# Second batch's long-chunk convolution moved to TensorE as diagonal products, its pointwise part ahead of the first q, k, v, and the third batch's taps next on VectorE

## The reference

```
h = depthwise_conv(x, w_dw, 7 taps, SAME) + b_dw        # along the tokens, channel by channel
h = relu(w_pw @ h + b_pw); h = max over token pairs     # 1024 -> 512 tokens
y = real(fft2(h)); h = layernorm(y) * gamma + beta      # "front"
n = layernorm(h)
q, k, v = n @ Wq.T, n @ Wk.T, n @ Wv.T                  # 12 heads of 16 dims
h = h + causal_linear_attention(taylor_exp(q), taylor_exp(k), v) @ Wo.T
n = layernorm(h)
h = h + top-1 mixture of 8 experts(n) + scan features over the 512 tokens
```

## Time and profile before

| | |
|---|---|
| timed runs | 442.24, 436.63, 442.59 us; median 442.24 |
| profiled execution, its own time | 429.96 us |
| span of its instructions | 428.2 us |
| TensorE busy | 373.9 us, 87% |
| VectorE busy | 271.1 us, 63% |
| ScalarE busy | 150.1 us, 35% |
| GpSimd busy | 91.2 us, 21% |
| mean granted TensorE clock | 0.937 |

### The profile page before, as it was taken

One profiled execution on the slowest core, in us unless ns is written; L12 is line 12 of the kernel. 1 busy time (PEld: TensorE's weight loads), 2 busy tenths in 40 slices (PEclk: granted clock), 3 DMA queues, 4 the chain that ended last, 5 costly groups with the idle time before them and its releaser, 6 DMA issues.

```text
span 428.2 us, 7994 instructions
## 1 busy us (share of the span) xinstructions
PE 373.9 (87%) x2820; PEld 265.8 (62%) x2821; DVE 271.1 (63%) x866; ACT 150.1 (35%) x299; POOL 91.2 (21%) x128
## 2 busy tenths in 40 slices
PE   7999899889898888988988997889799999998273
PEld 4486657436374354743665535689699899887252
DVE  6689703999198992987024386738556655565783
ACT  1010120773106732067434461354333443342000
POOL 1000000451003520034101241400634433341100
PEclk9999899999899999999996899969999999999656
DMA  8667120000300000086002001120241111113504
GB/s 269 196 215 263 44 55 0 2 2 2 100 0 2 1 2 2 0 331 210 2 2 86 2 2 73 51 61 2 83 141 43 53 45 51 46 51 56 165 3 147
DMA packets 21571, 30.58 MB, mean 71 GB/s; under 512 B 9876, under 2 KB 18132, under 8 KB 21028
## 3 DMA queue, kind: packets, MB, share of 16 engines
q1 hardware_dynamic: 17812, 24.02, 17.5%
q0 software_dynamic: 2208, 5.29, 4.3%
q10 hardware_dynamic: 1520, 0.86, 0.7%
HBM read 24.20 MB, written 5.96 MB: 70 GB/s over the span
## 4 chain that ended last, share of the span: by engine, by line
PE 66%; DVE 14%; ACT 7%; issue 5%; DMA 3%; POOL 3%; DVEq 0%; ACTq 0%; POOLq 0%
PE upper L1630 10%; PE ring L1616 7%; PE upper L1479 5%; PE ring L1463 4%; PE ring L1620 4%; ACT probs L639 4%; PE ring L1372 4%; POOL probs L569 3%; PE upper L1307 2%; PE ring L1378 2%; PE ring L1353 2%; PE ring L1319 2%; PE upper L1535 2%; PE upper L1396 2%; PE ring L1358 2%
## 5 line engine op out<-in xcount | busy, mean ns | idle before, releaser
L569 POOL TENSOR_SCALAR_AFFINE_SELECT probs<-probs 128x256 f32<-128x256 f32 (+1 forms) x72 | 43.4, 604 | 212.9 <-ACT probs L639 211.8
L639 ACT ACTIVATE probs<-ring,ones 128x768 f32<-128x768 f32 (+1 forms) x54 | 52.0, 995 | 23.3 <-PE ring L1463 16.9
L721 ACT ACTIVATE probs<-ring,qk 128x128 f32<-128x128 f32 x138 | 38.2, 378 | 55.4 <-PE ring L1620 30.2
L1630 PE MATMUL upper<-w,probs 128*128 x276 | 51.8, 339 | 3.1 <-DVE probs L1105 1.8
L1630 PEld LDWEIGHTS upper<-w,probs 128*128 128x128 f32 x276 | 46.1, 196 | 5.2 <-issue 4.9
L1479 PE MATMUL upper<-probs,va 128*32 128x512 f32 (+3 forms) x384 | 34.9, 459 | 12.6 <-POOL probs L569 12.6
L1463 PE MATMUL ring<-qk 32*128 32x512 f32 (+3 forms) x276 | 43.0, 520 | 3.1 <-ACT probs L639 3.1
L770 DVE SCALAR_TENSOR_TENSOR wide<-w,wdw,wide 128x512 f32<-128x512 f32 (+1 forms) x42 | 41.1, 1020 | 0.6
L585 POOL DMA_INDIRECT ffn_by_token<-probs,target x23 | 22.5, 979 | 72.3 <-DVE probs L1113 71.1
L1616 PE MATMUL ring<-xsT,qk 128*128 128x128 f32 x276 | 35.9, 280 | 0.6 <-ACT xsT L713 0.6
L1463 PEld LDWEIGHTS ring<-qk 32*128 32x128 f32 x276 | 19.9, 193 | 25.3 <-ACT probs L639 18.9
(11 more groups left out here) (324 smaller groups left out, 624.7 us busy)
## 6 DMA issues: line engine op xcount, KB each, us to landing
w<-in_w SPq DMA_DIRECT2D x1, 4608.0 KB, 15.8
w1a<-in_w1a SPq DMA_DIRECT2D x1, 3072.0 KB, 10.5
w<-in_x SPq DMA_DIRECT2D x4, 512.0 KB, 3.9
w<-in_x SPq DMA_DIRECT2D x8, 256.0 KB, 5.0
w1b<-in_w1b SPq DMA_DIRECT2D x1, 1536.0 KB, 13.8
tokens<-x_all SPq DMA_DIRECT2D x4, 384.0 KB, 8.7
x_all<-ffn_by_token SPq DMA_DIRECT2D x4, 384.0 KB, 5.0
wide<-scores_linear SPq DMA_DIRECT2D x1, 1024.0 KB, 5.3
```

Of the source, the lines that this page charges most:

```text
L569: nc.gpsimd.affine_select(diag, diag, heads + [[1, P]], ALU.is_ge, minus_one, base=0, channel_multiplier=-1).then_inc(p_ready, 1)
L639: nc.scalar.activation(squares(n), score_bank(b, n)[:, :, 0:unit_width(n)], ACT.Square, bias=ones[:, 0:1], scale=0.25).then_inc(sq_done, 1)
L721: nc.scalar.activation(hT[slot][:, c, :], ring[slot][:, c % 2, P * (c // 2):P * (c // 2) + P], ACT.Gelu_apprx_tanh, bias=b1_col[slot][:, c ...
L1630: last = nc.tensor.matmul(att[2][:, 0:D], hT[slot][:, c, :], w2[:, bass.ds((e * HC + c) * D, D)], start=(c == 0), stop=(c == HC - 1))
```

## The change

VectorE builds a second set of seven diagonal matrices (`taps_long`) while it waits for the first pointwise result. TensorE computes batch 1's long chunk as 14 diagonal products (seven taps by two halves of the tokens) into `ring[0]`, behind `transform(0)` and ahead of the short chunk's seven. ScalarE adds the bias and writes `conv`, and raises `conv_done` by two. Both halves of `convolve(1)` leave VectorE. `pointwise(1)` goes to the PSUM pairs of `upper` instead of `ring`, and stands ahead of `project(0)`; the 56 fillers become 8, the 20 behind `pointwise(1)` go. `convolve(2)` moves on VectorE from between two of batch 0's attention sums to right behind `pool(1)`.

```diff
+        def point_banks(b):
+            return (ring[0][:, :, :], ring[1][:, 0, :]) if b != 1 else (upper[:, 0:2, :], upper[:, 2, :])
...
-        taps = probs[:, 0:TAPS * P].rearrange("p (k c) -> p k c", k=TAPS)
+        taps, taps_long = (probs[:, TAPS * P * i:TAPS * P * i + TAPS * P].rearrange("p (k c) -> p k c", k=TAPS)
+                           for i in range(2))
...
-        WARM_PROJECT, WARM_EXPERTS, WARM_FEATURES, WARM_ROWS = 56, 32, 14, 10
+        WARM_EXPERTS, WARM_FEATURES, WARM_ROWS = 32, 14, 10
...  ScalarE
             def project(b):
                 if b == 0:
                     copy_taps(1)
+                    act.wait_ge(long_sums_done, 1)
+                    nc.scalar.activation(conv, ring[0][:, :, :].rearrange("p h n -> p (h n)"), ACT.Identity,
+                                         bias=vec2[:, 0, 0:1]).then_inc(conv_done, 2)
...  VectorE, pool(b)
+                if b == 0:
+                    nc.vector.tensor_tensor(taps_long, ident[:, None, :].to_broadcast([P, TAPS, P]),
+                                            wdw[:, 0, :, None].to_broadcast([P, TAPS, P]), ALU.mult
+                                            ).then_inc(long_taps_ready, 1)
                 dve.wait_ge(pw_done, 2 * b + 1)
...  VectorE
             def front(b):
                 pool(b)
-                if b == 0:
-                    convolve(1, (0,))
+                if b == 1:
+                    convolve(2)
                 if b >= 2:
                     add_attended(b - 2)
                     normalise_again(b - 2)
                 untangle(b)
                 normalise(b)
-                if b == 0:
-                    convolve(1, (1,))
-                else:
+                if b > 0:
                     sums(b - 1, 1)
-                    if b < B - 1:
-                        convolve(b + 1)
+                    if b == 2:
+                        convolve(3)
                     sums(b - 1, 2)
...  TensorE
             def pointwise(b):
-                if b > 0:
+                if b == 1:
+                    pe.wait_ge(tap_sums_copied, 2)
+                if b > 1:
                     pe.wait_ge(gh_copied, 2 * b)
...
             def transform(b):
...
+                if b == 1:
+                    pe.wait_ge(qk_copied, KEY_BLOCKS)
+                    pe.wait_ge(v_copied, 1)
                 pe.wait_ge(pool_done, 8 * b + 4)
...
+            def sum_long_taps():
+                pe.wait_ge(long_taps_ready, 1)
+                for tap in range(TAPS):
+                    for h in range(2):
+                        last = nc.tensor.matmul(ring[0][:, h, :], taps_long[:, tap, :],
+                                                xin[:, 0, tap + 512 * h:tap + 512 * h + 512],
+                                                start=(tap == 0), stop=(tap == TAPS - 1))
+                last.then_inc(long_sums_done, 1)
...
             transform(0)
             pe.wait_ge(s_x, 96)
+            sum_long_taps()
             sum_taps(1)
             pe.wait_ge(y_done, 1)
-            keep_clock(WARM_PROJECT)
+            keep_clock(8, misc)
+            pointwise(1)
             pe.wait_ge(s_wa, 16 * len(ATTN))
             project(0)
-            pointwise(1)
-            keep_clock(WARM_FOLD)
             transform(1)
             attend(0)
             project(1)
```

More of the change, by code:

```diff
@@ L331, in build @@
         conv_done = sem("conv_done")
+        long_taps_ready, long_sums_done = sem("long_taps_ready"), sem("long_sums_done")
         taps_ready, tap_sums_done, tap_sums_copied = sem("taps_ready"), sem("tap_sums_done"), sem("tap_sums_copied")
@@ L812, in pool @@
                     dve.wait_ge(col_done, 2 * b)
-                gather(pooled[:, :, 0:even_n], ring[0][:, :, :].rearrange("p h (n two) -> p h n two", two=2), 0)
+                long, short = point_banks(b)
+                gather(pooled[:, :, 0:even_n], long.rearrange("p h (n two) -> p h n two", two=2), 0)
                 for h in range(2):
@@ L816, in pool @@
                 dve.wait_ge(pw_done, 2 * b + 2)
-                gather(pooled_s[:, 0:even_n], in_pairs(ring[1][:, 0, :]), 1)
+                gather(pooled_s[:, 0:even_n], in_pairs(short), 1)
                 for h in range(2):
@@ L1317, in pointwise @@
                 pe.wait_ge(conv_done, 2 * b + 2)
+                long, short = point_banks(b)
                 for h in range(2):
-                    nc.tensor.matmul(ring[0][:, h, :], wpw[:, 0, 0:P], of_parity(conv, h), start=True, stop=False)
+                    nc.tensor.matmul(long[:, h, :], wpw[:, 0, 0:P], of_parity(conv, h), start=True, stop=False)
                 if b < 2:
@@ L1322, in pointwise @@
                 for h in range(2):
-                    last = nc.tensor.matmul(ring[0][:, h, :], wpw[rows_of(h), 1, 0:P], conv_s[rows_of(h), :],
+                    last = nc.tensor.matmul(long[:, h, :], wpw[rows_of(h), 1, 0:P], conv_s[rows_of(h), :],
                                             start=False, stop=True)
@@ L1326, in pointwise @@
                 for h in range(2):
-                    nc.tensor.matmul(ring[1][rows_of(h), 0, :], wpw[:, 0, P:D], of_parity(conv, h), start=True, stop=False)
+                    nc.tensor.matmul(short[rows_of(h), :], wpw[:, 0, P:D], of_parity(conv, h), start=True, stop=False)
                 for h in range(2):
-                    last = nc.tensor.matmul(ring[1][rows_of(h), 0, :], wpw[rows_of(h), 1, P:D], conv_s[rows_of(h), :],
+                    last = nc.tensor.matmul(short[rows_of(h), :], wpw[rows_of(h), 1, P:D], conv_s[rows_of(h), :],
                                             start=False, stop=True)
```

## The result

The changed kernel takes 445.24 us (median of four runs, 440.0 to 448.31) against 439.44 of the kernel before beside it (433.03 to 442.59): ratio 1.0197, 95% interval 1.0116 to 1.0277. The ratio leaves disturbed runs out, so it isn't the quotient of the medians. The forecast was 444.2, +0.5%.

The account below looks back on a forecast made before the run. TensorE was taken to bound the kernel, VectorE to wait. transform(1) 2.7 us late less 0.7 in attend(0) made 2.0 us slower, put on the timed median of 442.24: 444.2, range 435 to 451.

Parts of the forecast that it names:

- transform(1): TensorE's start of batch 1's transform: at 70.3 instead of 67.61, 2.7 us late.
- Long sums: TensorE behind transform(0): 28 counted products added on the path at 0.453 each, 12.7 us.
- The new wait: TensorE before pointwise(1), for ScalarE's two copies: 2.0 us, bounds 1.7 and 2.4, about 1.1 us of it idle.
- Pointwise: pointwise(1) on TensorE, moved ahead of project(0): 5.1 us, 52.2 to 57.3.
- project(0): TensorE behind pointwise(1): 13.05 us instead of 14.6, with 1.56 us of low clock regained.
- kept-dip rival: Clock dip stays in project(0), or one its size (1.56) comes in the pointwise part: 3.6 us slower, 445.8; chance 0.28.
- The slow rival: Clock falls at ScalarE's two copies, before pointwise(1), and stays low: 8.7 us slower, 450.9; chance 0.12.
- Taps of batch 2: convolve(2) on VectorE: 13.7 us, from 60.0 to 73.7, with 3.9 us margin at untangle(1).
- late-convolution rival: Batch 2's x lands more than 5.3 us late, pushing batch 1's normalisation on VectorE: 446 to 449; chance 0.03.
- attend(0): Batch 0's attention, without the convolution beside it: 0.69 us shorter, bounds 0 to 1.
- The faster rival: The timed runs' 12.3 us surplus is low clock between 31 and 68 and would go: 432; chance 0.07.

Follow-up runs that it names:

- e4: Changed kernel, but VectorE does tokens 0 to 511 of batch 1's long chunk, TensorE the rest as 7 products, long copy first; 431.10 us, 0.9932.
- e3: Changed kernel with ScalarE's two copies exchanged, the long chunk's copy ahead of the short one's; 433.16 us, 1.0030.
- e9: The kernel before, unaltered, run again under its own label with 12 runs; 431.52 us, 0.9977 of itself.
- e11: The kernel before with only convolve(2) moved right behind pool(1); 439.96 us, 1.0188.
- e5: Changed kernel with convolve(2) back in its old place on VectorE, between two of batch 0's attention sums; 437.15 us, 1.0099.
- the controls: Changed kernel and kernel before, each rerun unaltered; quotients of their ratios, changed against before, 1.002 and 1.008.
- e6: Changed kernel's new order without the long diagonal products: VectorE does both halves of batch 1's long chunk, TensorE runs 112 fillers; 1.0111.
- e2: The kernel before, unaltered, run under its own label with 6 runs; 436.42 us, 1.0110 of itself.
- e7: e4 with 16 more fillers in the expert logits, ahead of the last attention; 430.16 us, 0.9926.

## Why the prediction held, step by step

It held in its mechanism and, in the touched stretch, in its size: transform(1) later (2.1 us against before's profiled execution, 2.7 forecast), the attention shorter (22.59 against 23.38, 0.79; 0.69 forecast), +1.35 together, where 2.0 was forecast.

That the time came out at 445.24 for 444.2 is luck in good part. The forecast stood on a median of 442.24; the kernel before beside the changed one read 439.44, and 432.4 to 433.0 in the later comparisons. So the base moved by more than the change, and the first comparison showed +5.8 us between the medians, not +2.0.

- **Long sums**: 33.31 to 45.37, 12.06 us instead of 12.7. I had taken 0.453 from products whose source is two of every four elements; the long chunk's source is contiguous, and a counted instruction takes 0.431. e4's seven at 31.83 to 37.87 give the same. The strided ones stayed at 0.450 (45.37 to 51.67). That the stride is the reason is argued: the two groups also differ in weights and bank. The Trainium skill, "TensorE: Matmul & The Clock Gate", section "Wait — 56ns, not 53.3ns?", gives 215.7 ns from start to start for 512 columns at full clock; two of these are 0.431, so the trace agrees if a counted float32 instruction is two such passes.
- **The new wait**: 2.04 us, 1.00 of them idle; 2.0 and 1.1 forecast. e3 shows the cause of the 1.1 by removing it.
- **Pointwise**: 53.71 to 58.79, 5.08; 5.1 forecast.
- **project(0)**: 12.96 to transform(1); 13.05 forecast. But the argument was half wrong. I booked 1.56 us as regained from a dip "behind the 1.88 us of idleness". e9 has the same wait and no dip. The dip is a property of some executions; up to transform(1) the changed kernel costs 2.1 us against an execution with it and 3.7 against one without. The 3.7 is the kept-dip rival's size, but no whole front shows it: e9's dip comes later, in attend(0), and to the next q, k the changed kernel is 1.8 us behind e9 and 1.4 behind the other two. All three traces of the kernel before lose one dip somewhere in this stretch, and one of four changed traces does. Whether the change avoids it, or these executions happened to, so few traces don't show.
- **The slow rival** (clock falls at the new wait, 450.9): not seen. In all four changed traces the granted clock is 1.00 from 30 to 75 us, 2.4 GHz, with 1.00 us of idleness before the pointwise part. Where a wait of 4.81 us stood, e11, the clock did go to 0.50 and stayed for 13.7 us. The Trainium skill, "TensorE: Matmul & The Clock Gate", section "HAM oscillation — how this bites in real kernels", tells of a kernel in which long waits between blocks of products make each next block start slow. e11's row agrees; the waits of that kernel are longer than 1.00 us, so it doesn't speak of the changed kernel's. Between the two stands the wait of 1.87 us, with a fall behind it in two of three traces, and in e11 too: so I had been right to price it, and had no ground to say which way it would go.
- **Taps of batch 2**: 12.7 us instead of 13.7, since no mask contends; margin 5.00 instead of 3.9. e11 is what the late-convolution rival looks like, with the margin gone.
- **attend(0)**: without the convolution 0.41 us for a mask, with it 1.36 (e5) and 1.46. The Trainium skill, "SBUF — State Buffer", section "SBUF: two separate sides", has VectorE and GpSimd share a port pair, which one of them holds for a whole instruction, if VectorE reads two SBUF inputs and GpSimd's instruction reads SBUF as well. The tap's instruction reads two and the mask reads `probs`, and the rows agree.
- **The faster rival** (the timed surplus lies here): against it stand 38.3 us in four traces with no low clock in the stretch, and times no lower than before's beside them. The surplus was not of the kernel: the kernel before, unaltered, lost it in the later comparisons.

What I had not weighed is the size of what wanders: 1.6 us for each low stretch, 9.6 for a pace of the tiles. I take the first comparison's 1.0197 to contain some of it; the controls' 1.002 and 1.008 are nearer to what the stage shows. The exact percentage stays open within these.

## What to carry to other kernels

A shift of work from an idle engine to the busiest one costs its own length (12.06 us here, paid by fillers and a wait); shift only the part that the idle engine can't finish in time, and issue the copy of the part that is ready first. Before a dip or a gain of 1 to 2 us is put into a sum, look at a second execution of the same kernel: here the dip stood in two of three, and in the third it had moved. And run the old kernel under a label of its own beside the new one: its 1.011 against itself was as large as the change.

## What the runs showed of the hardware

- A counted float32 product of 512 columns takes 0.431 us with a contiguous source (28 in 12.06 us) and 0.450 in the group with a strided one (two of every four elements; 14 in 6.30 us).
- Idle time before a block and the clock behind it: 1.00 to 1.15 us, no fall in six of six traces (four changed, e5, e6); 1.87 us, a fall in three of four (before, e2, e11; not e9); 4.81 us, a fall during it and the low level for 13.7 us (one trace).
- The low level outlasts the wait by which it comes, with TensorE busy all of 5 us (270 to 275, above), and its stretches move between executions of one kernel: 53.6, 63.8 and 57.3 us in three traces of the kernel before.
- In two executions (the first changed one, and e7 for part of its tiles) TensorE's semaphore increments land late, by 0.64 to 1.16 us in the first, and a tile of the experts takes 5.2 us for 4.6. No run here shows why.
